# One wait for room per two groups of gathers, instead of one per group, in both graph passes of a four-layer graph network

## The reference, cut to what matters

```
# first block: attention over the edges, four heads
e = leaky_relu(a_src[src] + a_dst[dst]);  p = exp(e - max);  alpha = p / segment_sum(p, dst)[dst]
out = segment_sum(alpha[:, :, None] * h[src], dst)
# third block: a weighted sum over the same edges
messages = edge_val[:, None] * embeddings[edge_src]
neighbor_emb = segment_sum(messages, edge_dst)
```

## Time and profile before

| what | us |
|---|---|
| median of 3 runs (9080.73 to 9103.37) | 9087.52 |
| span of the profiled execution | 9073.9 |
| the rest of the median around that span | 13.6 |
| first pass, first to last gather issued | 202.7 to 2756.2 |
| second pass, first to last gather issued | 4301.8 to 6845.9 |
| PE busy / DVE busy / ACT busy / POOL busy, whole span | 5819.2 / 3938.2 / 1583.2 / 5476.3 |

### The profile page before, as it was taken

How to read it: one execution, slowest core, us unless ns; L and a number is a source line. 1 busy time by engine, 2 the same in 40 slices (tenths; PEclk the granted TensorE clock), 3 DMA queues, 4 the chain that set the end, 5 groups by cost and what they waited for, 6 DMA issues and landing times. The chain is left out here.

```text
span 9073.9 us, 116515 instructions
## 1 busy us (share of the span) xinstructions
PE 5819.2 (64%) x27644; PEld 4894.5 (54%) x27645; DVE 3938.2 (43%) x10109; ACT 1583.2 (17%) x3574; POOL 5476.3 (60%) x5690
## 2 busy tenths in 40 slices
PE   4677777777772488881444444444442579998984
PEld 3566665666662477771333333333331478888883
DVE  4566666777776400004444434434331532222225
ACT  1122222221220233330000000000000233333331
POOL 3566666666666466666666666666666246666662
PEclk7777777777775599995777777776765768888786
DMA  3333333333333144443333222222220022222345
GB/s 113 84 88 87 89 89 85 88 86 87 87 86 108 49 140 145 145 145 114 88 89 88 86 81 81 81 80 82 79 82 19 22 60 67 65 69 65 67 67 163
DMA packets 426058, 793.32 MB, mean 87 GB/s; under 512 B 129162, under 2 KB 267134, under 8 KB 425684
## 3 DMA queue, kind: packets, MB, share of 16 engines
q0 software_dynamic: 235504, 474.87, 21.0%
q1 hardware_dynamic: 190436, 317.20, 10.4%
HBM read 720.67 MB, written 70.98 MB: 87 GB/s over the span
## 5 line engine op out<-in xcount | busy, mean ns | idle before, releaser
L1147 PE MATMUL g_pM<-g_G,g_S 128*128 x3328 | 1178.4, 531 | 1570.5 <-DVE g_S L932 834.9
L831 POOL DMA_INDIRECT g_G<-table,X x1664 | 1620.8, 974 | 933.8 <-issue 447.1
L839 POOL DMA_INDIRECT g_G<-table,g_IDX x1616 | 1534.2, 949 | 863.9 <-issue 460.8
L1147 PEld LDWEIGHTS g_pM<-g_G,g_S 128*128 128x128 f32 x3328 | 903.1, 278 | 1845.8 <-issue 1652.9
L1115 PE MATMUL g_pM<-g_G,g_S 128*128 128x260 f32 x3328 | 1196.4, 499 | 593.1 <-DVE acc L944 555.7
L1691 POOL DMA_INDIRECT q_G<-table,slot x1072 | 1037.1, 967 | 591.5 <-issue 288.3
L618 POOL DMA_INDIRECT slots<-sort_PAIR,sort_ADDR x1024 | 1012.3, 989 | 521.4 <-issue 310.7
L952 DVE TENSOR_TENSOR acc<-g_pM,acc 128x256 f32 x1664 | 697.2, 419 | 1257.4 <-remote 693.1
L1115 PEld LDWEIGHTS g_pM<-g_G,g_S 128*128 128x128 f32 x3328 | 722.3, 238 | 906.4 <-DVE acc L944 647.2
L944 DVE TENSOR_TENSOR acc<-g_pM,acc 128x260 f32 x1664 | 711.4, 428 | 468.4 <-remote 204.0
L932 DVE TENSOR_SCALAR g_S<-iota,g_REL,g_WT 128x128 f32<-128x128 f32 x1664 | 588.8, 354 | 288.2 <-issue 259.2
(11 more groups left out here) (335 smaller groups left out, 7007.3 us busy)
## 6 DMA issues: line engine op xcount, KB each, us to landing
e_W<-in_L_ffn_W SPq DMA_DIRECT2D x210, 512.0 KB
sort_PAIR<-slot_rows SPq DMA_DIRECT2D x66, 512.0 KB
g_G<-table,X POOLq DMA_INDIRECT x1664
g_G<-table,g_IDX POOLq DMA_INDIRECT x1616
ys_all<-ew_Y SPq DMA_DIRECT2D x196, 128.0 KB
sm_Y<-ys_all SPq DMA_DIRECT2D x28, 896.0 KB, 10.5
q_ST<-slot_rows SPq DMA_DIRECT2D x34, 512.0 KB
sort_ADDR<-slot_rows SPq DMA_DIRECT2D x34, 512.0 KB
```

Of the source, the lines that this page charges most:

```text
L831: pool.indirect_dma_start(G[:, r, u, :], None, table, bass.IndirectOffsetOnAxis(ap=IDX[:, k * GRP + u:k * GRP + u + 1].bitcast(U32), axis= ...
L839: pool.indirect_dma_start(G[:, r, u, :], None, table, bass.IndirectOffsetOnAxis(ap=IDX[:, g * GRP + u:g * GRP + u + 1].bitcast(U32), axis= ...
L1147: m = pe.matmul(pM[r % 2 * 2 + half][:, u % HG, :], S[:, r, u, :], rows.rearrange("p a d -> p (a d)"), start=True, stop=True)
```

## The change

In the first pass POOL now waits only before groups of even number, and there for the sums of the group three before, which is the later of the two groups whose places the next sixteen gathers overwrite. In the second pass the wait before groups of odd number is dropped, and the wait before those of even number stays as it was.

```
             def step_attending(k):
...
-                if k >= RINGS:
-                    pool.wait_ge(s["part"], summed(k - RINGS, PAIRS - 1))
+                if k >= RINGS and k % 2 == 0:
+                    pool.wait_ge(s["part"], summed(k + 1 - RINGS, PAIRS - 1))
...
             def step_placing(g):
...
-                at_least(pool, s["room"], g - AHEAD + 1)
+                if g % 2 == 0:
+                    at_least(pool, s["room"], g - AHEAD + 1)
```

## The result

The changed kernel takes 9930.33 us (median of 4 runs, 9906.58 to 9936.92) against 9091.12 us: a ratio of 1.0922, 95% interval 1.0902 to 1.0943. It is 839 us slower. The forecast was 9555 with a range from 9060 to 9870, so the direction was right and the size was not. The profiled execution has a span of 9934.0 us.

What follows compares the result with a forecast made beforehand. POOL was taken to pace the first pass, its waits opening gaps for the other engines. 9073.9 + 408 (sixteen in a row) + 79 (second half) - 19 (second pass) = 9541.9, with 13.6 around the span 9555 us; range 9060 to 9870.

Steps and rivals of the forecast that it cites:

- What bounds the kernel, and the mechanism: First pass: POOL paces it; long gather runs stop the other engines' handshakes, and its 2.39 us waits open gaps.
- Waits removed, later release: First pass: 204 waits become 102, as mere toll 2.39 us less per pair; waiting for the later group costs nothing.
- Sixteen in a row: First pass: sixteen gathers per release make a pair 28.5 us against 24.5, +408 us over 102 pairs.
- open work: First pass: the part of a pair's time when the engines are not held up, taken as 20.0 us for two groups.
- closed part: First pass: time per pair when the other engines' handshakes stop during a long gather run, taken as 8.5 us.
- Second half: First pass, second half: DVE's extra 3.1 us per pair may come to the front, 0 to 158 us, 79 taken.
- Second pass: Second pass: POOL can only issue earlier; at most 99 waits left, gain 0 to 38 us, -19 taken.
- the upper case: First pass: stretch closes early and ends late, 12.2 us closed, 32.2 us per pair, +785 us; chance 0.08.
- The rival that gave 9930: First pass: the stretch closes as early as in the second pass, +785 instead of +408 us; chance 0.08.
- The signs: L831 waits about 102 of 8 us; DVE and PE gaps about 8 us per pair; first pass some 450 us longer.
- The toll: First pass: rival that held releases are only transfer latency paid per wait, gaining 214 us, total 8855; chance 0.14.
- The closed time follows the number of gathers: Rival: each gather closes the engines for a share of its time however grouped; time stays near 9088; chance 0.10.

Runs made afterwards that it cites:

- e4: Changed kernel, first pass only, with POOL waiting between the two groups of eight until its first group's gathers have landed; ratio 1.0005 to the kernel before.
- e14: Changed kernel, with POOL also waiting mid-group in both passes until its own four gathers have landed; ratio 0.9856 to the kernel before.
- e3: Kernel before, but in the first pass every group of eight waits for the sum of group k-3 instead of k-4; ratio 0.9998.
- e13: Kernel before, with POOL also waiting mid-group in both passes until its own four gathers have landed; ratio 0.9856.
- e2: Kernel before with only the edit of the second pass; 9111.11 us, ratio 1.0029.
- e6: Kernel before, with otherwise idle SP sending 64 increments nobody waits for after each group's sums in the first pass; 9742.57 us, ratio 1.0703.
- e9: Kernel before, with SP running 63 already satisfied waits and two signals after each group's sums in the first pass; ratio 1.0654.
- e7: Changed first pass, second as before, each gather fetching half a row per partition (520 bytes instead of 1040); 9921.54 us, one run.
- e8: Changed first pass, second as before, each gather fetching 64 rows instead of 128; 10225.08 us, one run.

## Why the prediction was right and wrong

**What bounds the kernel, and the mechanism: right.** The reading of the earlier trace rows, that POOL's wait buys a gap in its own stream, is what e4 and e14 show: give the gap back and the loss is gone.

**Waits removed, later release: right.** Fewer waits are worth nothing by themselves and the later event costs nothing (e3: 0.9998; e14: as fast as e13).

**Sixteen in a row: the step that failed.** The term was 20.0 us of open work + 8.5 closed = 28.5 us per pair, +408 us. Measured in the first half: 30.6 us. The closed part is what was too small. DVE's waits at the node sums, in the 50 pairs from 269.1 to 1799.4 and in the 51 from there to 3558.3 (us in total, times, longest):

```profile
DVE acc L945 <- remote: 544.6, 84, 11.6
...
DVE acc L945 <- issue: 64.1, 9, 9.6
```

```profile
DVE acc L945 <- remote: 591.8, 95, 10.3
...
DVE acc L945 <- issue: 43.4, 6, 10.3
```

That is 12.2 us closed per pair in the first half and 12.5 in the second, not 8.5. It leaves 18.4 us of open work in the first half, less than the 20.0 taken, although the step behind a stop can run at a granted clock of 0.50. In the one pair that the prediction had, the engines kept going for some 15 us of the run (to 268.87); in the regular course they first stop 7.6 to 9.0 us after the run's start (the middle 80% of the first half's pairs). The prediction's own doubt, that the 28.5 us might owe something to the pass having just started, is borne out by the changed kernel:

```profile
269.18 0.94 POOL L831 DMA_INDIRECT g_G<-table,X  x1 [19.21 <-PE g_pM L1116]
...
296.89 0.94 POOL L831 DMA_INDIRECT g_G<-table,X  x1 [8.00 <-PE g_pM L1116]
...
328.06 0.94 POOL L831 DMA_INDIRECT g_G<-table,X  x1 [11.45 <-PE g_pM L1116]
```

Its pair at that place takes 27.7 us with a wait of 8.00, the next one 31.2 us with 11.45. What is special about the start is not shown. It is not the length of POOL's pause ahead of the run, which the prediction named: in the regular course of the first half that pause is as long (10.9 us on the mean, 10.85 in the earlier trace rows). At 6.2 us instead of 4.0, 102 pairs make 636 us: 228 of the 371 us that were missing (839 measured less 468 forecast).

**Second half: mis-sized.** Half of 3.1 us per pair was taken, 79 us. A pair of the second half costs 3.6 us more beyond its own 0.3 in the kernel before, on 51 pairs 183 us: 104 more than predicted. The closed time is nearly the same in both halves, the open work goes from 18.4 to 22.0 us: the scan and the copy (2.34 + 1.29 us) come to the front whole.

**Second pass: wrong sign, small.** +15 us in the trace and 26.5 in e2, predicted -19: by the trace 34 of the missing 371. The 99 waits came as foreseen, at 3.97 us.

**The bounds.** The prediction itself wrote down +785 for the closed time and up to 158 for the second half, and then gave the upper case 0.08 because the pair at hand said 8.5. One pair at the start of a pass is weak evidence for 102. The range does not follow from its terms either: up to +750, up to 158 and -19 on 9087.5 reach 9977, and it was ended at 9870. The rival that gave 9930 had the closed time right: 12.2 us against 12.2 and 12.5 measured, though in two pieces and not in one. That its sum (9555 + 377, which is 9932) meets the median so closely is luck: it had 864 us for the first pass, which took 814 more, and -19 for the second, which took 15 more.

**The signs.** As foreseen: 102 waits at L831, unchanged durations of the instructions on POOL and DVE, a longer first pass, a second pass within 40 us, and in most pairs the end of the last stop: it comes 4.0 us after the sixteenth gather's issue in the median pair (4.19 in the pair shown, 1029.59 less 1025.40). Not as foreseen: the mean wait (12.9, not 8), the length of the gap, and that it is broken. In the pair shown DVE came back for a moment at 1025.23, 0.2 us before the sixteenth issue, so the stretch can open before the run has drained. The two halves do not show the same pair (30.6 and 34.5 us), so the second half's term was real.

**The other rivals.** The toll falls with the result: fewer waits, more time. The Trainium skill, "DMA: Bandwidth & Descriptors", section Anatomy of one DMA — SWDGE (gpsimd) path, which spoke for it, gives about 2.0 us of fixed cost; POOL's landing waits (2.07 to 2.09 us, counted from the end of the last gather's 0.95) agree. What it says besides, that many descriptors can be emitted before their cost shows, no run here contradicts for POOL itself (0.95 us a gather before and after); what a long stream costs here, it costs the other engines, and no run shows that the descriptors are the reason. "The closed time follows the number of gathers" falls too: the same 1664 gathers take 3367 or 2510 us, by their pauses alone.

## What to carry to other kernels

Where an engine issues a long stream of gathers, look at what the other engines do during it, not at the issuing engine's own waits: a wait may be the pause that lets them work, and taking it away moves its cost to them, several times over. If releases are made rarer, put the issuer's own pause in their place, for instance a wait for its last gathers to land, and put it where the release isn't due yet. A size that is read off a single stretch at the start of a pass need not hold in its regular course: here 8.5 us became 12.2 to 12.5.

## What the runs showed of the hardware that was not expected

- An idle engine is not free. 64 satisfied waits or signals per group on SP, for which nobody waits, made the kernel 7.0% and 6.5% slower; in e6 the first pass took 3238 us instead of 2553, and in the row of e9 DVE stops 3.4 us after the run's start instead of 8 to 9.
- Half the bytes per gather changed nothing (9921.54); half the rows made it slower (10225.08). Each is one run.
- After a stop of 9.5 us PE's granted clock was 0.50 for the next step, and 16 matmuls took 3.42 instead of 1.94 us.
- What the engines compete for stays open. SP's waits use it as much as SP's signals do, and the bytes show no part in it. The Trainium skill describes something of that kind, "NOTIFIC — the notification-queue block", section 7.1: inside, a block that records events holds its producers back rather than lose a record. e6, e7 and e9 fit this, e8 is not explained by it; no row or run shows the block. Each run here has a span and a granted clock on record, so none tells whether an execution that nobody records would be held up in the same way. That wasn't tried.
